# First attention of a Flamingo block: q bias carried by a freed row of Wq, score factor in the LayerNorm, weight rounding on GpSimd, VW fills spread over the steps

## The reference, cut to what matters

```
h = (x - mean(x)) / sqrt(var(x) + 1e-5)                 # LayerNorm, no weights
q = (h @ Wq + bq)            -> 8 groups of 4 heads, head size 128
k, v = split(ctx @ Wkv + bkv) -> 8 groups, 64 rows each
p = softmax(q k^T / sqrt(128))                          # 32 heads, over 64 context rows
x = x + tanh(g) * (concat(p v) @ Wo + bo)
```

## Time and profile before

| | |
|---|---|
| median of 3 runs | 1533.31 us (1529.5, 1533.31, 1533.53) |
| profiled execution | known by its span, 1532.8 us from the first to the last instruction |
| TensorE matmul | 1433.3 us busy, 94% |
| VectorE | 1135.0 us, 74% |
| ScalarE | 756.9 us, 49% |
| GpSimd | 517.1 us, 34% |
| mean granted clock of TensorE | 0.990 of full speed |
| first attention | the first 387 us of the span |

### The profile page before, as it was taken

One profiled execution on the slowest core, in us unless ns is written; L12 is line 12 of the kernel. 1 busy time (PEld: TensorE's weight loads), 2 busy tenths in 40 slices (PEclk: granted clock), 3 DMA queues, 4 the chain that ended last, 5 costly groups with the idle time before them and its releaser, 6 DMA issues. The chain is left out here.

```text
span 1532.8 us, 24378 instructions
## 1 busy us (share of the span) xinstructions
PE 1433.3 (94%) x8064; PEld 1209.6 (79%) x8064; DVE 1135.0 (74%) x2870; ACT 756.9 (49%) x2127; POOL 517.1 (34%) x586
## 2 busy tenths in 40 slices
PE   5999999999999998999999999999999999999889
PEld 4888888887778887787888878878878887877767
DVE  7888888888641426778788788787787787786765
ACT  5666666667220314545545554554555555455521
POOL 4733333443691722232132132132132222322110
PEclk9999999999999999999999999999999999999979
DMA  4111111120230300100101001001001001010001
GB/s 186 70 66 45 68 55 68 68 68 1 83 112 28 131 18 1 69 1 15 56 1 68 0 0 68 0 0 68 0 0 68 0 0 68 19 35 1 1 1 55
DMA packets 14933, 63.75 MB, mean 42 GB/s; under 512 B 1760, under 2 KB 1760, under 8 KB 10656
## 3 DMA queue, kind: packets, MB, share of 16 engines
q1 hardware_dynamic: 14880, 63.07, 11.6%
HBM read 60.97 MB, written 2.10 MB: 41 GB/s over the span
## 5 line engine op out<-in xcount | busy, mean ns | idle before, releaser
L1183 ACT ACTIVATE p<-psum,nb,rq 128x320 f32<-128x320 f32 x256 | 155.5, 614 | 208.1 <-DVE nb L997 208.0
L55 PE MATMUL psum<-w1q_hi,xnT_lo 128*128 128x512 f32 x256 | 108.9, 425 | 7.7 <-DVE v_lo L1017 4.3
L993 DVE TENSOR_REDUCE mx<-psum 128x2 f32<-128x640 f32 x128 | 105.0, 820 | 9.4 <-PE psum L57 3.8
L962 DVE TENSOR_TENSOR pT_lo<-psum,pT_hi 128x512 fp32r<-128x512 f32 x128 | 88.0, 688 | 26.1 <-ACT pT_hi L1126 24.0
L923 POOL TENSOR_TENSOR rk<-ssk,rms_eps 128x3 f32<-128x3 f32 x32 | 6.2, 195 | 296.6 <-DVE ssk L1031 296.6
L243 POOL TENSOR_TENSOR p<-p,rinv 128x256 f32<-128x256 f32 x64 | 39.2, 613 | 193.0 <-DVE rinv L319 193.0
L434 ACT ACTIVATE p<-psum,nb 128x64 f32<-128x64 f32 x256 | 76.8, 313 | 50.7 <-DVE nb L344 50.6
L56 PE MATMUL psum<-w1q_lo,xnT_hi 128*128 128x512 f32 x256 | 101.4, 396 | 0.0
L57 PE MATMUL psum<-w1q_hi,xnT_hi 128*128 128x512 f32 x256 | 101.2, 395 | 0.0
L55 PE MATMUL psum<-w1o_hi,oT_lo 128*128 128x512 f32 x256 | 100.9, 394 | 0.0
L56 PE MATMUL psum<-w1o_lo,oT_hi 128*128 128x512 f32 x256 | 100.6, 393 | 0.0
(11 more groups left out here) (249 smaller groups left out, 4827.5 us busy)
## 6 DMA issues: line engine op xcount, KB each, us to landing
raw_q<-in_w0q SPq DMA_DIRECT2D x8, 1024.0 KB, 4.8
raw_o<-in_w0o SPq DMA_DIRECT2D x8, 1024.0 KB, 4.8
raw_q<-in_w1q SPq DMA_DIRECT2D x8, 1024.0 KB, 7.6
raw_o<-in_w1o SPq DMA_DIRECT2D x8, 1024.0 KB, 4.9
raw_kv<-in_w_gu SPq DMA_DIRECT2D x10, 512.0 KB, 3.6
raw_gu<-in_w_gu SPq DMA_DIRECT2D x10, 512.0 KB, 3.6
raw_kv<-in_w0kv SPq DMA_DIRECT2D x8, 515.0 KB, 3.3
raw_kv<-in_w1kv SPq DMA_DIRECT2D x8, 512.0 KB, 5.6
```

The source lines that it names most:

```text
L55: pe.matmul(out, w[1], m[0], start=start, stop=False)
L962: last = dve.tensor_tensor(k.pT[1][:, kt, 2 * hp:2 * hp + 2, :], bank.rearrange("p (h q) -> p h q", h=2), f(k.pT[0][:, kt, 2 * hp:2 * hp + ...
L993: dve.tensor_reduce(k.mx[:, stat(j)], s_pair(j), AX.X, ALU.max).then_inc(mx_ready, 1)
L1183: last = act.activation(k.p1[:, tile, h, :], s_pair(j)[:, h % 2, :], ACT.Exp, bias=k.nb[:, i:i + 1], scale=k.rq[:, i:i + 1], accum_out=k.r ...
```

## The change

Six edits, all in the first attention and its LayerNorm:
1. The q bias. h sums to zero over its 512 features, so row 511 of Wq can be taken from every other row without changing h @ Wq, and is then free. It takes bq, and feature 511 of h is set to a constant. In the kernel's layout row 511 is the last column of each head of `raw_q`. The fill `bq`, the operands bqk, bq_rep and ones, and the 13th score matmul go. Added are, once a group, `q_last` (the negative of that column, GpSimd), the copy of bq into it, and the subtraction over 511 columns for each of four heads (ScalarE, `q_shift`, in steps 1 to 4).
2. The score factor 1/sqrt(128) goes into the LayerNorm's reciprocal root, so the negative maximum is one instruction.
3. The rounding copies of the next group's weights move from VectorE to GpSimd, in pieces, with the subtractions; GpSimd waits for the data itself.
4. The fill `kv` is split in two, k and v, and is in step 7 instead of 6.
5. All eight VW fills belong to the running group: two in step 0, one in each of steps 1 to 6. The WK fills are 3, 3 and 2 in steps 8 to 10. The head has no VW fill.
6. In step 0 VectorE does its two VW fills before the maximum.

```diff
     def pool_rstd(self, pool, c, t):
-        pool.tensor_scalar(k.ln_rs[:, t:t + 1], k.ln_mv[:, t, 1:2], LN_EPS, None, ALU.add)
+        pool.tensor_scalar(k.ln_rs[:, t:t + 1], k.ln_mv[:, t, 1:2], LN_EPS, float(HD) if c == 0 else 1.0, ALU.add, ALU.mult)
...
-    NEXT_PREP = {6: [("kv",)], 8: [("wk", 0), ("wk", 1), ("wk", 2), ("bq",)], 9: [("wk", 3), ("wk", 4), ("vw", 0, 0)],
-                 10: [("wk", 5), ("wk", 6), ("wk", 7), ("vw", 1, 0)]}
-    OWN_PREP = {0: [("vw", 2, 0), ("vw", 3, 0)], 1: [("vw", 0, 1)], 3: [("vw", 1, 1)], 4: [("vw", 2, 1)], 5: [("vw", 3, 1)]}
+    OWN_PREP = {0: [("vw", 0, 0), ("vw", 1, 0)], 1: [("vw", 2, 0)], 2: [("vw", 3, 0)], 3: [("vw", 0, 1)],
+                4: [("vw", 1, 1)], 5: [("vw", 2, 1)], 6: [("vw", 3, 1)]}
+    NEXT_PREP = {7: [("kv", 0), ("kv", 1)], 8: [("wk", 0), ("wk", 1), ("wk", 2)], 9: [("wk", 3), ("wk", 4), ("wk", 5)],
+                 10: [("wk", 6), ("wk", 7)]}
...
+    def bias_copy(eng):
+        return eng.tensor_copy(k.bias[:, :], k.raw_kv[:, KVW:KVW + GH + 2])
+
+    def q_last_row(eng):
+        return eng.tensor_scalar(k.q_last[:, :].unsqueeze(2), raw_q4[:, :, LAST], -1.0, None, ALU.mult)
...
     def gpsimd(pool):
+        def hi_piece(kind, i):
+            s = piece(kind, i)
+            return pool.tensor_copy(wts[kind][0][:, s], raw[kind][:, s]).then_inc(hi_of[kind], 1)
...
+        def next_ready(g, t):
+            if t == 0:
+                pool.wait_ge(kv_in, 16 * g + 16)
+                pool.wait_ge(q_in, 16 * g + 16)
+                pool.wait_ge(prep_free, HEAD + FILLS * (g - 1))
+            elif 2 <= t < 6:
+                pool.wait_ge(q_shifted, CONV["q"] * g + t - 1)
+            elif t == 6:
+                pool.wait_ge(o_in, 16 * g + 16)
+                pool.wait_ge(prep_full, HEAD + FILLS * (g - 1) + ORDER.index(("vw", 1, 1)) + 1)
+            elif t == 7:
+                pool.wait_ge(prep_full, HEAD + FILLS * (g - 1) + ORDER.index(("vw", 3, 1)) + 1)
+
+        def next_split(g, t):
+            if t == 0:
+                bias_copy(pool).then_inc(bias_in, 1)
+                q_last_row(pool).then_inc(q_row_set, 1)
+                hi_piece("kv", 0)
+                hi_piece("kv", 1)
+            elif t == 1:
+                lo_piece("kv", g, 0)
+                lo_piece("kv", g, 1)
+            elif t < 6:
+                hi_piece("q", t - 2)
+                lo_piece("q", g, t - 2)
+            else:
+                heads = (0, 1) if t == 6 else (2, 3)
+                for h in heads:
+                    hi_piece("o", h)
+                for h in heads:
+                    lo_piece("o", g, h)
 
         def body(g, nxt):
             for t in range(NT):
+                if nxt:
+                    next_ready(g + 1, t)
                 pool.wait_ge(p_rec, NT * g + t + 1)
                 p = by_head(k.p0[:, t % 4, :])
                 pool.tensor_tensor(p, p, spread(k.rinv0[:, t % 4, :]), ALU.mult).then_inc(p_ready, 1)
                 if nxt:
-                    for kind, i in sched.get(t, []):
-                        lo_piece(kind, g + 1, i)
-                    if t == 2:
-                        bq_rows(g + 1)
+                    next_split(g + 1, t)
...
     def vector(dve):
+        def head_q():
+            dve.wait_ge(q_in, 16)
+            q_last_row(dve).then_inc(q_row_set, 1)
+            dve.wait_ge(q_row_set, 1)
+            dve.wait_ge(bias_in, 1)
+            dve.tensor_copy(raw_q4[:, :, LAST], k.bias[:, 0:GH].unsqueeze(2))
+            for h in range(GH):
+                last = dve.tensor_scalar(raw_q4[:, h, 0:HID - 1], raw_q4[:, h, 0:HID - 1], k.q_last[:, h:h + 1], None, ALU.add)
+            last.then_inc(q_shifted, CONV["q"])
...
+                fills = steps_fills(s, nxt)
+                if s == 0:
+                    for fill in fills:
+                        prep(base, fill)
                 if s < NT:
                     dve.wait_ge(s_full, n + 1)
-                    dve.tensor_reduce(k.mx0[:, s % 2, :], by_head(s_bank[s % 2][:, 0:GH * CTX]), AX.X, ALU.max)\
-                       .then_inc(s_max, 1)
-                    dve.wait_ge(s_max, n + 1)
-                    dve.tensor_scalar(k.nb0[:, s % 2, :], k.mx0[:, s % 2, :], -SCALE, None, ALU.mult).then_inc(nb_ready, 1)
-                for fill in steps_fills(s, nxt):
-                    prep(base, fill)
+                    dve.tensor_reduce(k.nb0[:, s % 2, :], by_head(s_bank[s % 2][:, 0:GH * CTX]), AX.X, ALU.max,
+                                      negate=True).then_inc(nb_ready, 1)
+                if s > 0:
+                    for fill in fills:
+                        prep(base, fill)
...
-                if nxt and s in (1, 3, 5):
-                    conv({1: "kv", 3: "q", 5: "o"}[s], g + 1)
...
     def scalar(act):
+        def q_shift(g, h):
+            if h == 0:
+                act.wait_ge(q_row_set, g + 1)
+                act.activation(raw_q4[:, :, LAST], k.bias[:, 0:GH].unsqueeze(2), ACT.Copy)
+            act.activation(raw_q4[:, h, 0:HID - 1], raw_q4[:, h, 0:HID - 1], ACT.Identity,
+                           bias=k.q_last[:, h:h + 1]).then_inc(q_shifted, 1)
...
                     last.then_inc(p_exp, 1)
+                if nxt and 1 <= s <= GH:
+                    q_shift(g + 1, s - 1)
...
     def tensor(pe):
                     for c in range(CH):
-                        mm3(pe, S, [w[:, c, s * PART:(s + 1) * PART] for w in k.xnT],
-                            [w[:, c, b, :, :] for w in k.WK], c == 0, False)
-                    pe.matmul(S, k.ones[:, :], k.bqk[:, b, :, :], start=False, stop=True).then_inc(s_full, 1)
+                        last = mm3(pe, S, [w[:, c, s * PART:(s + 1) * PART] for w in k.xnT],
+                                   [w[:, c, b, :, :] for w in k.WK], c == 0, c == CH - 1)
+                    last.then_inc(s_full, 1)
```

More of the change, by code:

```diff
@@ L107, in act_norm @@
             act.wait_ge(self.turned, m - 1)
-        act.activation(k.xn_tok[:, t % 2, :], k.x[:, t, :], ACT.Identity, bias=k.ln_nb[:, t:t + 1],
+        n = HID - 1 if c == 0 else HID
+        act.activation(k.xn_tok[:, t % 2, 0:n], k.x[:, t, 0:n], ACT.Identity, bias=k.ln_nb[:, t:t + 1],
                        scale=k.ln_rs[:, t:t + 1]).then_inc(self.xn, 1)
@@ L155, in attn0_phase @@
     LN_TILES = 4
-    HEAD_ORDER = [("kv",), ("bq",)] + [("wk", j) for j in range(8)] + [("vw", 0, 0), ("vw", 1, 0)]
-    FREE0 = 2
+    HEAD_ORDER = [("kv", 0), ("kv", 1)] + [("wk", j) for j in range(8)]
     CONV = {"kv": 2, "q": 4, "o": 4}
+    LAST = slice(HID - 1, HID)
     wq4, wo4 = [by_head(w[:, :]) for w in k.w_q], [by_head(w[:, :]) for w in k.w_o]
@@ L161, in attn0_phase @@
     ctx4 = [w[:, :].rearrange("p (c n) -> p c n", c=CH) for w in k.ctxT]
+    raw_q4 = by_head(k.raw_q[:, :])
     s_bank, pt_bank, o_bank = [k.bank[3], k.bank[4]], k.bank[5], [k.bank[6], k.bank[7]]
@@ L264, in gpsimd @@
                            ALU.subtract).then_inc(ctx_lo, 1)
-        bq_rows(0)
+        pool.wait_ge(ctx_lo, 1)
+        pool.memset(k.xn_tok[:, :, LAST], SCALE).then_inc(xn_one, 1)
         for t in range(NT):
@@ L298, in prep @@
             if kind == "kv":
[L299 to L305, removed]
+                j = fill[1]
+                last = dve.scalar_tensor_tensor(
+                    out=k.kvT[1][:, j, :], in0=bank[:, 0:BATCH * CTX], scalar=k.bias[:, GH + j:GH + j + 1],
+                    in1=f(k.kvT[0][:, j, :]), op0=ALU.add, op1=ALU.subtract)
             elif kind == "wk":
@@ L365, in vector @@
         dve.tensor_copy(k.ctxT[0][:, :], k.xn_tok[:, :, :].rearrange("p a b -> p (a b)")).then_inc(ctx_hi, 1)
[L366 to L372, removed]
+        head_kv()
+        head_q()
         dve.wait_ge(in_small, 48)
@@ L377, in vector @@
                                  op0=ALU.mult, op1=ALU.mult)
[L378 to L383, removed]
+        prep(None, ("kv", 0))
+        prep(None, ("kv", 1))
+        for t in range(3):
+            stats(t)
         for t in range(NT):
@@ L389, in vector @@
             if t == 5:
[L390 to L392 removed]
+                head_o_hi()
         body(0, True)
@@ L405, in prep @@
             if kind == "kv":
[L406 to L411, removed]
+                j = fill[1]
+                last = act.activation(k.kvT[0][:, j, :], bank[:, 0:BATCH * CTX], ACT.Identity,
+                                      bias=k.bias[:, GH + j:GH + j + 1])
             elif kind == "wk":
@@ L426, in body @@
                 for fill in steps_fills(s, nxt):
+                    if fill[0] == "kv" and fill[1] == 0:
+                        act.wait_ge(bias_in, g + 2)
                     prep(base, fill)
@@ L473, in prep @@
             if kind == "kv":
-                pe.wait_ge(kv_lo, CONV["kv"] * (g + 1))
-                for j in range(2):
-                    for c in range(CH):
-                        last = mm3(pe, bank[:, j * 256:(j + 1) * 256], [w[:, c, j * HD:(j + 1) * HD] for w in wkv4],
```

(18 more changed lines are left out.)

82 lines of the change are left out of this document (34 added, 48 removed).

## The result

The changed kernel takes 1543.15 us (median of four runs, 1542.61 to 1544.21) against 1533.22 for the one before, measured beside it: ratio 1.0065, 95% interval 1.0052 to 1.0077. It is slower. The forecast was 1527.7, faster. The two profiled executions have spans of 1532.8 and 1540.8 us.

| phase | before, us | after, us | difference |
|---|---|---|---|
| head and first attention | 387.54 | 377.00 | -10.5 |
| feed-forward | 194.1 | 192.9 | -1.2 |
| second attention | 896.5 | 916.3 | +19.7 |
| experts | 54.6 | 54.6 | 0.0 |

A forecast was written before the change was run, and what follows sets the result against it. TensorE was taken to bound the first attention, with waits for VectorE and ScalarE. Terms -2.4 - 12.2 + 1.0 + 8.0 gave -5.6 us from 1533.3: 1527.7 us, likeliest case 1523 to 1532, all cases 1514 to 1537.

The forecast's parts named there:

- The sum: Whole kernel: head -2.4, seven groups -12.2, last group +1.0, clock falls +8.0, together -5.6 us; nothing for later phases.
- The 0.13 for slower: Chance given to a slower kernel; includes ScalarE pacing steps 1 to 4 through a dear q shift, itself 0.09.
- GpSimd and tail cases: First attention: GpSimd copies make p late, 1531.5 us, chance 0.07; or tail waits stay, 1528 or 1536, chance 0.09.
- Long stretch: Loop group from tile 1's transposes to the next step 0 scores: 34.82 us falls to 30.8, waits costed at zero.
- that rival: Half of the long stretch's 2.4 us of TensorE waits stays: 8.4 us worse in all; chance 0.09.
- Refill: Loop group from step 0 scores to tile 1's transposes: 9.52 us grows to 11.8, with two TensorE waits.
- both releasers: Tile 0's exponentials end the 1.15 us wait before step 2 scores; pT_lo ends the 2.3 before tile 1's transposes.
- those two rivals: Shift from 1.1 us makes the kernel slower, chance 0.09; GpSimd copies at 1.29 us delay p, 1531.5, chance 0.07.
- The group: One first-attention loop group takes 42.6 us, 1.74 less than 44.34; over seven groups -12.2 us before clock effects.
- Last group: Final first-attention group, without the shift: refill 1.7 us longer, 0.7 of waits and bias work gone; +1.0 (0 to 2).
- Head: Before group 0's scores: two fewer VW fills ahead, less a 0.7 us push from raw_q preparation; -2.4 (-3.1 to -1.5).
- The clock: Idle of 2.3 us in refills drops TensorE's clock in five of seven, 1.6 us each: +8.0 (0 to 12).

The follow-up runs named there:

- 16 memsets: Changed kernel with 16 idle one-column memsets put at the very start of VectorE's program; 1544.59 us, 1.0074 of the kernel before.
- 60 memsets: Changed kernel with 60 idle one-column memsets put at the very start of VectorE's program; 1522.93 us, 0.9933 of the kernel before.
- the run with the old addresses: Changed kernel with the unused constant tiles ones_f and ones still allocated, so later tiles keep the earlier SBUF addresses; 1544.47 us, 1.0060 of the kernel before.
- with 30: Changed kernel with 30 idle one-column memsets put at the very start of VectorE's program; 1522.54 us, 0.9925 of the kernel before.
- 110 memsets: Changed kernel with 110 idle one-column memsets put at the very start of VectorE's program; 1544.34 us, 1.0075 of the kernel before.
- 22 of them: Changed kernel with 22 idle one-column memsets put at the very start of VectorE's program; 1541.40 us, 1.0056 of the kernel before.

## Why the prediction was wrong, point by point

**The step that failed** is in its first lines: "because the change touches one phase only". The sum then took all that lies behind the first attention as it was. The code there is as it was; its place is not. The five stalls make the second attention 20.7 us longer (915.4 with 16 memsets, 894.8 with 60), 4.1 us a jump: between the same two runs TensorE's wait for that v_lo grows from 4.3 to 16.7 us in all, which is 2.5 us a jump, and the remaining 1.7 I put down to the clock, which falls to 0.50 behind each of these waits. No run held the clock up with the stall in place, but two turns had about half of the fall. With 16 memsets the mean clock over the 12 us from 788 is 0.86, and this turn takes 111.9 us from jump to jump; behind the other four jumps it is 0.72, and those turns take 112.6 to 112.9. The fourth turn of the run with the old addresses is the same: 0.86 and 111.9 us, against 112.7 to 113.0. Twice that difference of 0.6 to 1.1 us, as an estimate, agrees with the 1.7; a turn without a stall takes 108.5. Without the stalls the change is worth -10.8 to -11.8 us (the runs with 60 and with 30 against before), twice the -5.6 forecast and inside the range. The 0.13 for slower was for ScalarE and for parts of the GpSimd and tail cases, all of them in the first attention.

The Trainium skill (Runtime: NRT & Kernel Launch, section "Instruction fetch mechanics") has the mechanism: instructions come in blocks by the sequencer's own transfers, read ahead in order only, and a taken branch to a block that is no longer held waits for its fetch. The runs agree with that. They differ in the size: the Trainium skill gives two blocks of 16 KiB, 256 instructions each, by which the changed kernel and the same with 110 memsets could not both have stalled; both did. I did not weigh that section, and neither the diff nor a wait in the profile of before points to it. What could have been done is the count: VectorE loses 43 instructions ahead of a loop whose body is 309 long.

**Long stretch**: forecast 30.8 us, measured 252.99 - 222.52 = 30.5. Its waits went to nothing, as worked; so that rival fell.

**Refill**: forecast 11.8 us with waits of 1.15 and 2.3 idle; measured 11.7, with 0.96 and 2.20. The mechanism and both releasers were right, and the experiments bear out the edits blamed for them (VW_lo ahead of the maximum, the shift ahead of the VW copy). The shift was priced at 0.8 and took 0.74; GpSimd's copy at 0.8 (half-way between its two bounds is 0.89) and took 0.61, and p was late nowhere, so those two rivals fell. Rows by line, 40 to 380 us, answering to the earlier trace rows:

```profile
L459 ACT ACTIVATE raw_q<-raw_q,q_last 128x511 f32<-128x511 f32 x28 | 20.6, 736 | 0.0
```

```profile
L237 POOL CAST w0q_hi<-raw_q 128x512 fp32r<-128x512 f32 x28 | 17.1, 612 | 0.0
```

**The group**: 42.15 us against a forecast of 42.6, so 7 x 2.19 = 15.3 us less for seven instead of 12.2, ahead of the clock. **Last group**: 377.00 less its scores at 340.42 is 36.6 us, 36.1 before: +0.5 instead of +1.0. **Head**: 39.61 against 38.7, -1.5 instead of -2.4, at the end of its bounds. The four additions took 0.42 us each and pushed the kvT_lo row by 0.55, near the 0.7 taken. What the sum left out is the clock in the head: over 36 to 41 us it averaged 0.66, where it was 1.00 before, and the six VW matmuls ahead of the scores are 0.43 us apart instead of 0.23, 2.7 us in all.

```profile
36.89 0.80 PE L55 MATMUL psum<-w0o_hi,kvT_lo 128*128 128x512 f32 x1 [1.58 <-DVE xnT_lo L130]
37.48 0.63 PE L56 MATMUL psum<-w0o_lo,kvT_hi 128*128 128x512 f32 x1
```

With 60 memsets the same wait is 1.59 us, the clock stays at 1.00 and the scores start at 39.00.

**The clock**: five falls of 1.6 us were forecast. Four of the seven groups took 43.7 us instead of 42.2: 6.2 us. With it the parts come to -1.5 - 15.3 + 0.5 + 6.2 = -10.1 us, of the -10.5 measured (the first of the groups took only 41.6). The same wait went both ways, as the two refills above show: behind 222.52 the clock stays, behind 264.66 it falls.

```profile
222.00:226.00 4.00, 3.48 (x21) 3.10 (x22) 2.92 (x7) 3.94 (x15) 2.46 (x3) 1.00 0.41 132
264.00:268.00 4.00, 3.34 (x10) 2.67 (x11) 2.89 (x8) 3.96 (x15) 2.53 (x4) 0.67 0.41 132
```

So a count between none and all was right, and the length of the idle stretch alone, which the prediction took to decide at about 2 us, does not: 2.20 and 2.19 went different ways, and so did 1.58 and 1.59 in the head. The Trainium skill (TensorE: Matmul & The Clock Gate, section "HAM oscillation — how this bites in real kernels") has a kernel whose waits put the clock back every time. Those are DMA waits, longer than the ones here, and of the refill waits here four of seven did so.

## What to carry to other kernels

Before an edit that adds or removes instructions, look for hardware loops further on in the same engine's program and count their bodies; when a phase that was not edited changes its time, compare the packets of the instruction queue first, and move the program with instructions that run while the engine waits anyway. Then judge the edit: here a gain of 11 us and a loss of 21 had separate causes, the work of the edits and the number of their instructions. And the waits of 2.2 us on TensorE were worth more here than their length, since shortening them to 1.5 us also saved the clock.

## What the runs showed of the hardware

- VectorE's instructions came in packets of 8,192 bytes, 128 instructions, and the runs fit four of them being held: the body of 309 instructions was not read again in any turn from the three starts at which it touches three blocks (4, 17, 34), and was read in every turn, five packets each, from the five at which it touches four (84, 97, 102, 118, 124).
- A jump back to a block that was not held stopped VectorE for 2.3 to 2.6 us; with the block's end four instructions behind the target a second stop of 1.7 to 1.9 us followed.
- Eight one-column memsets, run while VectorE waited for data, decided over 18.9 us of 1541 (22 of them against 30).
